# Product-key stage: one-hots of tile 0 placed between the top-k of tile 0 and the top-k of tile 1

## The reference

```python
q = (x @ Wq + bq).reshape(-1, N_HEADS, D_KEYS)
q1, q2 = (q[..., :HALF], q[..., HALF:])
s1 = jnp.einsum('bhc,hnc->bhn', q1, keys[:, 0])
s2 = jnp.einsum('bhc,hnc->bhn', q2, keys[:, 1])
s1t, i1 = lax.top_k(s1, TOP_K)
s2t, i2 = lax.top_k(s2, TOP_K)
all_scores = (s1t[..., :, None] + s2t[..., None, :]).reshape(-1, N_HEADS, TOP_K * TOP_K)
all_idx = (i1[..., :, None] * N_KEYS + i2[..., None, :]).reshape(-1, N_HEADS, TOP_K * TOP_K)
scores, best = lax.top_k(all_scores, TOP_K)
indices = jnp.take_along_axis(all_idx, best, axis=-1)
w_d = w_down[indices]
w_u = w_up[indices]
inner = jnp.einsum('bd,bhkd->bhk', x, w_d)
vals = jax.nn.relu(inner) * jax.nn.softmax(scores, axis=-1)
out = jnp.einsum('bhk,bhkd->bd', vals, w_u)
```

## Time and profile before

| what | value |
| --- | --- |
| median of 3 runs | 1306.53 us (1305.01 to 1313.27) |
| span of the profiled execution | 1321.3 us |
| mean granted TensorE clock in it | 0.938 |
| product-key stage in it, first top-k to last add to h | 399.1 to 834.6 us |
| VectorE busy in it | 1019.1 us |

### The profile page before, as it was taken

The page is one execution under the profiler, slowest core; times in us unless marked ns, Lnnn a source line. Parts: engine busy times, 40 slices in busy tenths (PEclk is TensorE's granted clock), DMA queues, the critical chain, the costliest instruction groups (busy, mean ns, idle before and its releaser), DMA issues.

```text
span 1321.3 us, 24093 instructions
## 1 busy us (share of the span) xinstructions
PE 1074.0 (81%) x7848; PEld 824.4 (62%) x7848; DVE 1019.1 (77%) x3123; ACT 685.7 (52%) x1453; POOL 497.8 (38%) x464
## 2 busy tenths in 40 slices
PE   4169579486687888898898887889899898989997
PEld 3056456455554777777787787555566565766675
DVE  3379577596788999999999995487585875854687
ACT  1158476484674344344434423387584774826332
POOL 7337255273461443434425334064261542620000
PEclk9579889798898899999999999899999999998999
DMA  3030000000000000000000001200000000000000
GB/s 111 20 128 1 0 1 0 0 0 0 0 2 1 1 2 2 1 2 2 1 2 2 2 1 41 80 1 1 0 0 0 0 0 0 1 1 1 1 8 24
DMA packets 6425, 14.63 MB, mean 11 GB/s; under 512 B 1855, under 2 KB 4482, under 8 KB 5762
## 3 DMA queue, kind: packets, MB, share of 16 engines
q1 hardware_dynamic: 5314, 11.42, 2.5%
q0 software_dynamic: 1024, 2.10, 0.6%
HBM read 12.47 MB, written 1.05 MB: 10 GB/s over the span
## 4 chain that ended last, share of the span: by engine, by line
issue 33%; PE 31%; DVE 27%; POOL 5%; ACT 4%; DVEq 1%; POOLq 0%; DMA 0%; ACTq 0%; SPq 0%
PE quad L1420 4%; PE bank L1415 4%; PE quad L1140 4%; DVE a_eT L734 4%; DVE w_v L957 4%; DVE i L874 4%; PE quad L1152 3%; PE quad L1318 3%; POOL wu L351 2%; PE bank L1329 2%; DVE one_u L963 2%; PE bank L1262 2%; POOL a_en L369 1%; DVE bi L895 1%; PE bank L1298 1%
## 5 line engine op out<-in xcount | busy, mean ns | idle before, releaser
L369 POOL TENSOR_TENSOR a_en<-a_e,a_rrec 128x512 f32<-128x512 f32 x256 | 265.6, 1042 | 300.8 <-DVE a_rrec L728 287.2
L462 ACT ACTIVATE a_e<-bank,a_negmax 128x512 f32<-128x512 f32 x256 | 176.2, 689 | 61.8 <-DVE a_negmax L721 51.2
L721 DVE TENSOR_REDUCE a_negmax<-bank 128x1 f32<-128x512 f32 x256 | 176.0, 690 | 41.8 <-PE bank L1355 25.4
L1140 PE MATMUL quad<-ident,a_en 128*128 128x128 f32 x1024 | 164.0, 284 | 46.5 <-DVE a_eT L734 39.2
L1140 PEld LDWEIGHTS quad<-ident,a_en 128*128 128x128 f32 x1024 | 109.9, 143 | 139.4 <-issue 124.4
L404 POOL TENSOR_TENSOR vals<-relu_in,g_sb 128x512 f32<-128x512 f32 x80 | 125.0, 1603 | 153.6 <-DVE one_u L963 119.6
L1152 PE MATMUL quad<-a_eT,a_v 128*128 128x512 f32 x512 | 174.3, 431 | 0.3 <-DVE a_eT L734 0.3
L734 DVE TENSOR_TENSOR a_eT<-quad,a_eT 128x512 fp32r<-128x512 f32 x256 | 172.2, 675 | 2.6 <-ACT a_eT L471 2.5
L1298 PE MATMUL bank<-xnT,wd 128*128 128x128 f32 x1024 | 137.6, 291 | 35.3 <-ACT relu_in L554 35.2
L471 ACT CAST a_eT<-quad 128x512 fp32r<-128x512 f32 x256 | 148.0, 578 | 17.5 <-PE quad L1140 17.5
L1298 PEld LDWEIGHTS bank<-xnT,wd 128*128 128x128 f32 x1024 | 127.3, 201 | 43.8 <-ACT relu_in L554 43.5
(11 more groups left out here) (213 smaller groups left out, 1887.7 us busy)
## 6 DMA issues: line engine op xcount, KB each, us to landing
wd<-in_pk_down SPq DMA_DIRECT2D x1, 2048.0 KB, 8.1
wu<-in_pk_up SPq DMA_DIRECT2D x1, 2048.0 KB, 12.6
wu<-in_moe_w SPq DMA_DIRECT2D x2, 1024.0 KB
out<-h SPq DMA_DIRECT2D x4, 256.0 KB, 2.3
wd<-in_num_rows SPq DMA_DIRECT2D x1, 512.0 KB
q_st<-in_pk_wqT SPq DMA_DIRECT2D x1, 512.0 KB
q_st<-in_pk_keys SPq DMA_DIRECT2D x1, 512.0 KB
wd<-in_a_wq SPq DMA_DIRECT2D x1, 512.0 KB
```

What stands on the lines that cost most here:

```text
L369: nc.gpsimd.tensor_tensor(m.en[:, s % 3, :], m.e[:, s % 3, :], m.rrec[:, s % 4:s % 4 + 1].to_broadcast([P, S]), ALU.mult).then_inc(a.nr, 1)
L462: nc.scalar.activation(m.e[:, s % 3, :], bank[LOGITS[s % 3]][:, :], ACT.Exp, bias=m.negmax[:, s % 4:s % 4 + 1], accum_out=m.rowsum[:, s % ...
L721: V.tensor_reduce(m.negmax[:, s % 4:s % 4 + 1], bank[LOGITS[s % 3]][:, :], AX.X, ALU.max, negate=True).then_inc(a.mx, 1)
L1140: last = tp(bank[2 + s % 2][:, c * P:(c + 1) * P], m.en[:, s % 3, c * P:(c + 1) * P], ident[:])
```

## The change

The one-hots of tile 0, both halves of one_v and `one_hots(0)`, are issued in the first loop, right behind the top-k of tile 0 and ahead of the top-k of tile 1. The round of tile 0 then begins with `weigh(0, 1)`. The other rounds and the other engines are as before.

```diff
                 positions(t)
                 expert_numbers(t)
-            one_v_half(0, 0)
-            one_v_half(0, 1)
+                if t == 0:
+                    one_v_half(0, 0)
+                    one_v_half(0, 1)
+                    one_hots(0)
 
             for t in range(NT):
-                one_hots(t)
+                if t:
+                    one_hots(t)
                 weigh(t, 1)
                 if t:
                     ffn_residual(t - 1)
```

## The result

| | before | changed |
| --- | --- | --- |
| median | 1306.36 us (17 runs, 1299.9 to 1313.55) | 1315.06 us (17 runs, 1310.65 to 1319.93) |
| ratio, 95% interval | | 1.0058 (1.0041 to 1.0074) |
| span of the profiled execution | 1321.3 us | 1311.1 us (1312.91 with what lies around it) |

The changed kernel is slower by 0.58%, which is 7.6 us (5.4 to 9.7); the forecast was 7.4. The two medians by themselves lie 8.7 us apart, inside that interval. The two spans stand the other way round, and that is no contradiction: the profiled execution of before reached the first top-k only at 399.12 us, that of the changed kernel at 378.71. The 20.4 us lie in front of all that the change touches, in the first 90 us, where in the one execution of before ScalarE waited 22.3 us for its first copy of keyw. So both traces are compared from the first top-k instruction on.

A forecast was written before the change was run, and what follows sets the result against it. The prediction took time in this stage to be lost where VectorE stands still or TensorE starts late on what VectorE needs. Waits of 7.7 us less 0.3 from POOL gave +7.4 us on 1306.5, so 1313.9 us, range 1309 to 1319.

The forecast's parts named there:

- The first wait: In front of tile 0's one_v, VectorE stands 4.35 us until ScalarE has copied uv and psp.
- The second wait: In front of tile 0's first weigh, VectorE stands until TensorE's spread, queued behind tile 1's transposes, is through; 3.42 us.
- POOL's earlier start: POOL's first product of tile 0 starts earlier against the weigh, so veps and pair_s stretch less; 0.3 us gained.
- The sum: Whole kernel: 7.7 us later at the first weigh, less 0.3 from POOL, gives 7.4 us slower.
- 2.6 to 4.3 us in front of the weigh: Sign that the forecast is right: VectorE idle this long before tile 0's first weigh, released by TensorE.
- a weigh 7 to 8.6 us later: Sign that the forecast is right: tile 0's first weigh this much later against the top-k of tile 0.
- shifts as a whole: Behind tile 0's first weigh, engine orders stay as now, so everything after moves together and later rounds keep their length.
- The spread did not run beside tile 1's top-k: Rival, only the first wait counts: TensorE reaches tile 0's spread during tile 1's top-k; +4.3 us, 1310.8; chance 0.06.
- The clock gave nothing back: Rival, not slower: TensorE's clock stays up in later rounds and saves 10.85 us; −3.4 us, 1303.1; chance 0.04.
- It did not stay low either: Rival, much slower: TensorE's clock stays at 1.2 GHz through tile 0's round; about +25 us, 1331; chance 0.05.

The follow-up runs named there:

- one_v alone: Against the changed kernel, only tile 0's two one_v halves stay ahead of tile 1's top-k, w_v and one_u behind it; 7.7 us above before, 7.0 when run again.
- filled: Against the changed kernel, first half of tile 1's top-k placed ahead of tile 0's one-hots; 2.6 us above before (0.5 to 4.6).
- early copies: Against the changed kernel, tile 0's uvp transposes ahead of the last three inner-product groups, ScalarE's copies ahead of the last three Relus; 2.7 us above before.
- the kernel without either: Against the changed kernel, half of tile 1's top-k ahead of tile 0's one-hots, half of tile 0's spread ahead of tile 2's scores; 0.8 us above before.
- early spread: Against the changed kernel, first half of tile 0's spread and its copies ahead of tile 2's scores; 6.7 us above before, 8.2 when run again.

## Why the prediction was right

**The first wait** was forecast at 4.35 us and measured at 4.10. The difference is not in the wait's end: the last write of uvp, from whose end the wait counts, took 0.55 us here and 0.28 before. From the start of that write one_v came 4.65 us later (391.90 to 396.55), by the forecast 4.68. The wait is there without the second (one_v alone), it goes when VectorE has other work (filled), and it shrinks to 1.44 when the transposes and copies stand earlier in their queues (early copies): the cause named, two engines' queues ahead of the copies, is the cause.

**The second wait** was forecast between 2.58 and 4.27 us, and the middle, 3.42, was taken; it was 2.42. The cause was right: with the spread ahead of tile 2's scores in TensorE's queue it is gone. Its size was off by 1.0 us, and 2.42 lies just under the lower bound. It was off because the middle between the two clocks was taken: the scores of tile 2 ran at the low clock as they did before, but it rose at their end, and the transposes (0.40) and the spread (2.10) had the short times. The Trainium skill's rule that sustained work releases the clock (TensorE: Matmul & The Clock Gate, section "What's actually happening") was on the right side here; with it alone the forecast of this term would have been 2.58.

**POOL's earlier start** was to give 0.3 us. POOL's first product now starts 0.31 us ahead of the weigh instead of 0.11, veps shrank from 0.89 to 0.71, but pair_s grew from 1.50 to 1.71. These rows answer to the earlier trace rows:

```profile
421.56 4.52 POOL L404 TENSOR_TENSOR vals<-relu_in,g_sb 128x512 f32<-128x512 f32 x3 [2.27 <-ACT g_sb L590]
...
423.87 0.71 DVE L697 TENSOR_SCALAR veps<-mv 128x4 f32<-128x4 f32 x1
...
428.68 1.71 DVE L879 TENSOR_TENSOR pair_s<-m 128x512 f32<-128x512 f32 x1
```

What veps gained, pair_s gave back. It ends 0.55 us behind the end of the second of POOL's next two products, and that end, which hangs on ScalarE's copy of TensorE's third group, lies 7.96 us behind the weigh here and 7.95 before:

```profile
426.82 3.01 POOL L404 TENSOR_TENSOR vals<-relu_in,g_sb 128x512 f32<-128x512 f32 x2 [0.74 <-ACT g_sb L593]
```

The term is 0, not 0.3.

**The sum** at the first weigh was 7.7 by the forecast and 6.6 in the trace; with the 0.3 taken off, the forecast was 7.4, and the head of the stage came out 6.6 longer. Nearly all that is missing is the second wait. The time moved by 7.6 (5.4 to 9.7), so the forecast of the whole was closer than its terms, and that closeness is luck. Two of the forecast's own signs were missed on the low side: 2.6 to 4.3 us in front of the weigh (2.42), and a weigh 7 to 8.6 us later (6.6). That the rest "shifts as a whole" holds for eight rounds to 0.5 us. Behind them the two profiles part by 2.5 more. All the rounds from the first add to the last took 371.0 us before and 374.0 here, but 370 to 374 over the eleven profiles of changed kernels, 374.1 in one without either wait: a scatter of the rounds, which the time of this kernel shares.

That the loss as a whole hangs on the two waits is shown by the kernel without either: its one-hots stand between the top-ks, and its time is that of before (0.8 above, −1.3 to 3.0).

**The rivals.** The spread did not run beside tile 1's top-k, as the order of the queue said. The clock gave nothing back: it was 0.98 over the next eight rounds in both traces. It did not stay low either: 1.00 from 421.9 on.

**What stays open.** The kernels with a whole first wait and no second one cost 5.5 to 8.2 us in time, where their profiles show the weigh 3.8 to 4.4 late. For the early spread part of the rest is seen in the profile (up to 3.4 us behind the first weigh, by late and slow scores of tile 3). For one_v alone it is not: 7.7 and 7.0, against 4.4 by theory and 4.9 and 4.0 at the first add. Nor do the times of the changed kernel (7.6) and of one_v alone (7.7) differ as their heads do. The medians of the same runs do: they lie 8.7 us above before for the changed kernel, 6.4 and 5.9 for one_v alone, and 5.3 and 6.7 for the early spread. So a part of what is open is in how a few scattered runs are put into one number. The intervals are 2 to 3 us wide to each side, and the split of the 7.6 into 4.1 and 2.4 rests on the profiles.

## What to carry to other kernels

An engine that has no hole gains no time of its own when its work is moved earlier; the move only changes what hides what. Ahead of such a move, look up in the *other* engines' queues when the moved work's inputs come, and whether the engine that takes its results can reach them before its own next wait: here the inputs came 4 us too late and the taker stood behind another wait. And a block that looks like a delay (10 us of one-hots ahead of the weigh) may be the cover of the next engine's work.

## What the runs showed that was not expected

**The same work takes 0 to 4 us longer in the head, by TensorE's clock alone.** Up to the sum of the exponentials of tile 0 all kernels are alike on TensorE, but for the early copies, which come later. In before the granted clock was 1.00 there, in the filled kernel 0.50, with TensorE busy for 3.33 of the 4 us just ahead in both; two stretches of before, then the same two of the filled kernel:

```profile
399.10:403.10 4.00, 3.33 (x19) 2.44 (x18) 3.94 (x35) 0.59 (x1) 0.00 (x0) 1.00 0.00 0
403.10:411.10 8.00, 7.03 (x42) 5.30 (x41) 7.54 (x52) 3.80 (x9) 0.01 (x1) 1.00 0.00 0
```

```profile
379.70:383.70 4.00, 3.33 (x17) 2.45 (x16) 3.96 (x36) 0.59 (x1) 0.00 (x0) 0.89 0.00 0
383.70:391.70 8.00, 7.64 (x17) 4.40 (x17) 5.71 (x43) 0.85 (x2) 0.00 (x0) 0.50 0.00 0
```

The scores of tile 1 then come late, ScalarE takes the exponential behind them, and VectorE waits 4.16 us instead of 0.30 for it. It was 2.0 to 4.2 us in seven of twelve profiles, and in these seven the first pair of tile 1's scores took 1.66 to 2.08 us, in the other five 1.12 or 1.13. Why the clock falls in one execution and not in another is not shown. Two single profiles can thus differ by 4 us with nothing changed up to there, more than one of the waits that were looked for.

**An instruction of VectorE can lose to POOL more than once.** pair_s takes 0.67 us alone and 1.3 to 1.8 in about half of the rounds, beside POOL's products of 1.5 us each. In one round of the changed kernel it took 2.44, and that round was 1.5 us longer:

```profile
661.02 2.44 DVE L879 TENSOR_TENSOR pair_s<-m 128x512 f32<-128x512 f32 x1
```

That is 1.77 us over its own time, more than one of POOL's products is long. POOL's row of that time shows why:

```profile
655.37 7.54 POOL L404 TENSOR_TENSOR vals<-relu_in,g_sb 128x512 f32<-128x512 f32 x5 [9.19 <-DVE one_u L963]
```

POOL's five products ran without a gap to 662.91, and pair_s, begun at 661.02, ended 0.55 us behind them: it stood for the rest of the fourth product and for all of the fifth. Two other profiles have such a round (2.59 and 2.88 us), each ending 0.55 us behind a second product. In the rounds of 1.34 to 1.39 it ends 0.55 us behind the first, and POOL's next product takes about 2 us instead of 1.5. What decides who comes next is not shown. The Trainium skill (SBUF — State Buffer, section "SBUF: two separate sides") has the port pair locked for a whole instruction. The ends of these instructions agree with it.
